# The first attention's K and V products in five passes of 128 and 64 rows in place of six of 96

## The reference, cut to what matters

```python
x = x + _L0_xattn_ref(_layernorm(x), ctx_768, Wq, bq, Wk, bk, Wv, bv, Wo, bo)
# in _L0_xattn_ref: 16 heads of 16 channels, Nkv = 361
q = (query @ Wq + bq).reshape(B, Nq, H, D).transpose(0, 2, 1, 3)
k = (key_value @ Wk + bk).reshape(B, Nkv, H, D).transpose(0, 2, 1, 3)
v = (key_value @ Wv + bv).reshape(B, Nkv, H, D).transpose(0, 2, 1, 3)
attn = jnp.clip(jnp.einsum('bhqd,bhkd->bhqk', q, k) * scale, -CLAMP, CLAMP)
attn = jax.nn.softmax(attn, axis=-1)
attn = jnp.where(jnp.any(jnp.isnan(attn)), 1.0 / Nkv, attn)
x = jnp.einsum('bhqk,bhkd->bqhd', attn, v).reshape(B, Nq, Cq) @ Wo + bo
```

## Time and profile before

| | |
|---|---|
| median of 3 runs | 946.31 us (946.12 to 947.51) |
| the profiled execution | 947.37 us |
| its span, first to last instruction | 945.5 us |
| PE busy in the span | 792.7 us (84%) |
| DVE, ACT, POOL busy | 708.9, 559.2, 298.9 us |
| mean granted clock of TensorE | 0.910 of full speed |

### The profile page before, as it was taken

One profiled execution on the slowest core, in us unless ns is written; L12 is line 12 of the kernel. 1 busy time (PEld: TensorE's weight loads), 2 busy tenths in 40 slices (PEclk: granted clock), 3 DMA queues, 4 the chain that ended last, 5 costly groups with the idle time before them and its releaser, 6 DMA issues.

```text
span 945.5 us, 22076 instructions
## 1 busy us (share of the span) xinstructions
PE 792.7 (84%) x8198; PEld 582.7 (62%) x8198; DVE 708.9 (75%) x1450; ACT 559.2 (59%) x1159; POOL 298.9 (32%) x258
## 2 busy tenths in 40 slices
PE   3777888889898768999889999997655999769994
PEld 2455666666665645777657777784213887459994
DVE  8678777877877888777476666654796998677866
ACT  6666666666665436634365555536897776673542
POOL 6166444444441506040232220002730221342400
PEclk9699999999999776999999999997557999789998
DMA  6423444344452246515076554455210000200002
GB/s 169 108 70 86 113 96 99 103 97 114 119 121 81 80 138 222 175 35 145 23 222 188 170 168 146 124 135 142 75 42 11 1 1 1 90 1 2 2 2 70
DMA packets 76898, 89.53 MB, mean 95 GB/s; under 512 B 22150, under 2 KB 64929, under 8 KB 76826
## 3 DMA queue, kind: packets, MB, share of 16 engines
q1 hardware_dynamic: 69994, 80.50, 30.6%
q0 software_dynamic: 6144, 7.42, 3.0%
q10 hardware_dynamic: 688, 0.66, 0.3%
HBM read 72.87 MB, written 15.43 MB: 93 GB/s over the span
## 4 chain that ended last, share of the span: by engine, by line
PE 53%; DVE 26%; ACT 9%; issue 8%; POOL 2%; DMA 1%; ACTq 0%; DVEq 0%; POOLq 0%
PE ps L1207 11%; PE ps L1194 10%; PE ps L581 4%; PE ps L379 3%; PE ps L477 3%; PE ps L551 3%; DVE p L567 3%; PE ps L623 3%; PE ps L532 2%; PE ps L2229 2%; DVE m L537 2%; PE ps L2240 2%; DVE pmax L1681 1%; ACT area L2039 1%; PE ps L1728 1%
## 5 line engine op out<-in xcount | busy, mean ns | idle before, releaser
L537 DVE TENSOR_REDUCE m<-ps 100x2 f32<-100x722 f32 x128 | 115.6, 904 | 51.6 <-PE ps L532 49.7
L558 ACT ACTIVATE p<-ps 128x800 f32<-128x800 f32 x128 | 106.8, 834 | 41.6 <-PE ps L551 38.6
L1256 ACT ACTIVATE hT<-ps,cols 128x500 f32<-128x500 f32 (+1 forms) x96 | 62.5, 651 | 103.3 <-PE ps L1194 103.1
L1263 DVE TENSOR_TENSOR hT_l<-hT,hT_h 128x500 f16<-128x500 f32 (+1 forms) x96 | 62.4, 652 | 59.1 <-ACT hT_h L1257 59.1
L567 DVE SCALAR_TENSOR_TENSOR p<-p 128x600 f32<-128x600 f32 x128 | 106.6, 834 | 0.0
L1207 PE MATMUL ps<-w_h,hT_h 128*125 128x256 f16 (+1 forms) x384 | 104.7, 273 | 1.8 <-DVE x L1303 1.2
L1207 PE MATMUL ps<-w_h,hT_l 128*125 128x256 f16 (+1 forms) x384 | 104.7, 273 | 0.0
L1207 PE MATMUL ps<-w_l,hT_h 128*125 128x256 f16 (+1 forms) x384 | 104.7, 273 | 0.0
L1099 POOL DMA_INDIRECT xe<-tokens,slot_of x32 | 43.2, 1349 | 151.4 <-PE ps L1217 102.1
L1194 PE MATMUL ps<-xe_h,w_h 128*128 128x500 f16 (+1 forms) x192 | 73.3, 382 | 15.8 <-DVE xe_l L1237 5.5
L551 PE MATMUL ps<-qs,ks 128*128 128x100 f16 x768 | 63.3, 212 | 14.7 <-ACT p L558 14.7
(11 more groups left out here) (348 smaller groups left out, 2101.6 us busy)
## 6 DMA issues: line engine op xcount, KB each, us to landing
sw<-in_L_ffn_w_dram SPq DMA_DIRECT2D x16, 512.0 KB, 6.8
sw<-in_L_ffn_w_dram SPq DMA_DIRECT2D x8, 1024.0 KB, 5.8
k_parts<-kp SPq DMA_DIRECT2D x32, 192.0 KB, 2.2
ks<-k_parts SPq DMA_DIRECT2D x32, 192.0 KB
stage<-in_L_xattn_W_f_dram SPq DMA_DIRECT2D x6, 1024.0 KB, 7.5
ctx_f<-in_ctxT_dram SPq DMA_DIRECT2D x16, 270.8 KB, 3.2
stage<-in_ctxT_dram SPq DMA_DIRECT2D x8, 541.5 KB, 8.6
area<-in_ctxT_dram SPq DMA_DIRECT2D x16, 270.8 KB, 6.1
```

The costliest lines, as they stand in the source:

```text
L537: v.tensor_reduce(m32[p][:, 2 * i:2 * i + 2], ps[0:T, at:at + 2, 0:KV], AX.X, ALU.max).then_inc(m_max, 1)
L558: s.activation(p32[:, i % HALF, :, :, :].rearrange("p j n t -> p n j t"), ps[:, t_bank(i):t_bank(i) + 2, 0:(KJ + 1) * T].rearrange("p n (j ...
L1256: s.activation(hT[:, f % 3, 0:m], bank[2 + f % 2][:, 0:m], ACT.Silu, bias=bias, scale=1.0 / WS)
L1263: v.tensor_tensor(hTp[p][1][:, f, 0:m], hT[:, f % 3, 0:m], hTp[p][0][:, f, 0:m], ALU.subtract).then_inc(f_l, 1)
```

## The change

The 192 channels are cut into 128 and 64 in place of 96 and 96. The first 128 keep a high tile `ctxh[p][:, 0, :]` and a low tile `ctxl[p]`. The last 64 are loaded twice, into rows 0 to 63 and 64 to 127, and the tile `ctxh[p][:, 1, :]` holds their high part in the upper and their low part in the lower half of its rows; with the last 64 rows of the weights' high part standing twice as well, one pass of 128 rows makes high by high and high by low. Low by high for these channels is a pass of its own, over rows 0 to 63. That makes five passes: four of 128 rows and one of 64.

To write both halves of that tile with one subtraction, ACT writes the rounded copy into the lower rows of a tile `ctx_rest` alone, whose upper rows DVE sets to zero at the start; POOL subtracts it from the f32 value. As there is one `ctx_rest` for both buffers, `c_scalar` now waits for POOL's subtractions of the batch before. The guard's products take all 128 rows for the first part and rows 64 to 127 for the second. Wk, Wv and the context come in two transfers each, and the counts that wait for them double.

```diff
-        for name, rows_ in (("Wq", 128), ("Wk", KC), ("Wv", KC), ("Wo_heads", 128)):
+        for name, rows_ in (("Wq", 128), ("Wk", 128), ("Wv", 128), ("Wo_heads", 128)):
-        ctxp = [[sba(f"ctx{n}{p}", [KC, 2, KV], F16) for n in "hl"] for p in range(2)]
+        ctxh = [sba(f"ctxh{p}", [128, 2, KV], F16) for p in range(2)]
+        ctxl = [sba(f"ctxl{p}", [128, KV], F16) for p in range(2)]
+        ctx_rest = sba("ctx_rest", [128, KV], F16)
...
+        REST = CK - 128
+        def lower_rows(w):
+            return w[128:CK, :][None, :, :].broadcast_to((2, REST, C))
+        def ctx_terms(w, p):
+            hi, lo = w
+            return ((hi[:, 0, :], ctxh[p][:, 0, :]), (lo[:, 0, :], ctxh[p][:, 0, :]), (hi[:, 1, :], ctxh[p][:, 1, :]),
+                    (hi[:, 0, :], ctxl[p][:, :]), (lo[0:REST, 1, :], ctxh[p][0:REST, 1, :]))
...
-            for k in range(2):
-                for i, j in TERMS:
-                    mm = pe.matmul(at[:, 0:KV], wk[i][:, k, c * 128:(c + 1) * 128], ctxp[p][j][:, k, :],
-                                   start=(n == 0), stop=(n == 5))
+            for n, (w, src) in enumerate(ctx_terms(wk, p)):
+                mm = pe.matmul(at[:, 0:KV], w[:, c * 128:(c + 1) * 128], src, start=(n == 0), stop=(n == 4))
...
-                for k in range(2):
-                    for i, w in TERMS:
-                        mm = pe.matmul(at[0:v_rows(j), j % 2 * C:(j % 2 + 1) * C],
-                                       ctxp[p][i][:, k, j * AT:j * AT + v_rows(j)], wv[w][:, k, :],
-                                       start=(j != 1 and n == 0), stop=(n == 5), skip_group_check=True)
+                for n, (w, src) in enumerate(ctx_terms(wv, p)):
+                    mm = pe.matmul(at[0:v_rows(j), j % 2 * C:(j % 2 + 1) * C], src[:, j * AT:j * AT + v_rows(j)], w,
+                                   start=(j != 1 and n == 0), stop=(n == 4), skip_group_check=True)
...
             if c == 0:
-                s.wait_ge(ctx_in[p], 16 * (t + 1))
+                s.wait_ge(ctx_in[p], 32 * (t + 1))
                 wait(s, v_mm, 2 * (b - 1))
-            s.activation(ctxp[p][0][:, c, :], ctx_f32[p][:, c, :], ACT.Copy,
-                         accum_out=ctx_sum[:, c, bass.ds(b, 1)]).then_inc(c_h, 1)
+            else:
+                wait(s, c_l, 2 * b)
+            of = slice(0, 128) if c == 0 else slice(REST, 128)
+            high = ctxh[p][:, 0, :] if c == 0 else ctx_rest[of, :]
+            s.activation(high, ctx_f32[p][of, c, :], ACT.Copy, accum_out=ctx_sum[of, c, bass.ds(b, 1)]).then_inc(c_h, 1)
...
-            g.tensor_tensor(ctxp[p][1][:, c, :], ctx_f32[p][:, c, :], ctxp[p][0][:, c, :], ALU.subtract).then_inc(c_l, 1)
+            high = ctxh[p][:, 0, :] if c == 0 else ctx_rest[:, :]
+            parts = ctxl[p][:, :] if c == 0 else ctxh[p][:, 1, :]
+            g.tensor_tensor(parts, ctx_f32[p][:, c, :], high, ALU.subtract).then_inc(c_l, 1)
...
-            sp.dma_start(ctx_f32[p][:, :, :], ctx_d[b] ...).then_inc(ctx_in[p], 16)
+            sp.dma_start(ctx_f32[p][:, 0, :], ctx_rows[b][0:128, :]).then_inc(ctx_in[p], 16)
+            sp.dma_start(ctx_f32[p][:, 1, :], ctx_rows[b][128:CK, :][None, :, :].broadcast_to((2, REST, KV))
+                         ).then_inc(ctx_in[p], 16)
...
             for n in range(H):
                 row_ = HR * (n % 4)
                 for k in range(2):
+                    of = slice((0, REST)[k], 128)
                     mm = pe.matmul(UB_[row_:row_ + D, n // 4 * B:(n // 4 + 1) * B],
-                                   w_in_["Wv"][0][:, k, n * D:(n + 1) * D], ctx_sum[:, k, :],
+                                   w_in_["Wv"][0][of, k, n * D:(n + 1) * D], ctx_sum[of, k, :],
...
+            v.memset(ctx_rest[0:REST, :], 0.0)
             vs.inc(v.memset(eps_col[:, :], LN_EPS))
...
+                    s.dma_start(raw[:, 0, :], src[0:128, :]).then_inc(w_in[name], 16)
+                    s.dma_start(raw[:, 1, :], lower_rows(src)).then_inc(w_in[name], 16)
```

More of the change, by code:

```diff
@@ L149, in bias_row_tensor @@
         def bias_row_tensor(pe, part):
-            pe.wait_ge(wvo_in, 32)
+            pe.wait_ge(wvo_in, 48)
             for k in range(2 * part, 2 * part + 2):
@@ L250, in build @@
         ctx_raw = sba("ctx_f32", [128, 2, 2, KV])
-        ctx_f32 = [ctx_raw[0:KC, p, :, :] for p in range(2)]
-        ctxp = [[sba(f"ctx{n}{p}", [KC, 2, KV], F16) for n in "hl"] for p in range(2)]
+        ctx_f32 = [ctx_raw[:, p, :, :] for p in range(2)]
+        ctxh = [sba(f"ctxh{p}", [128, 2, KV], F16) for p in range(2)]
+        ctxl = [sba(f"ctxl{p}", [128, KV], F16) for p in range(2)]
+        ctx_rest = sba("ctx_rest", [128, KV], F16)
         k32 = [sba(f"k32_{c}", [128, KV]) for c in range(CC)]
@@ L290, in build @@
         qk_sum = sba("qk_sum", [128, 4, B])
-        ctx_sum = sba("ctx_sum", [KC, 2, B])
+        ctx_sum = sba("ctx_sum", [128, 2, B])
         guard = sba("guard", [128, 4])
@@ L315, in build @@
         ctx_d = a["ctxT"].rearrange("(c p) (b k) -> b p c k", c=2, b=B)
+        ctx_rows = a["ctxT"].rearrange("c (b k) -> b c k", b=B)
+        REST = CK - 128
[5 more added lines that the diff above has]
+                    (hi[:, 0, :], ctxl[p][:, :]), (lo[0:REST, 1, :], ctxh[p][0:REST, 1, :]))
         TERMS = ((0, 0), (0, 1), (1, 0))
@@ L353, in split_weight @@
             else:
-                v.wait_ge(w_in[name], 16)
+                v.wait_ge(w_in[name], 32)
                 vs.inc(v.tensor_scalar(hi, src, WS, None, ALU.mult))
@@ L375, in k_tensor @@
             turn_free(pe, free)
-            n = 0
-            for k in range(2):
-                for i, j in TERMS:
-                    mm = pe.matmul(at[:, 0:KV], wk[i][:, k, c * 128:(c + 1) * 128], ctxp[p][j][:, k, :],
-                                   start=(n == 0), stop=(n == 5))
-                    n += 1
+            for n, (w, src) in enumerate(ctx_terms(wk, p)):
+                mm = pe.matmul(at[:, 0:KV], w[:, c * 128:(c + 1) * 128], src, start=(n == 0), stop=(n == 4))
             mm.then_inc(k_mm, 1)
@@ L646, in c_scalar @@
             if c == 0:
-                s.wait_ge(ctx_in[p], 16 * (t + 1))
+                s.wait_ge(ctx_in[p], 32 * (t + 1))
                 wait(s, v_mm, 2 * (b - 1))
-            s.activation(ctxp[p][0][:, c, :], ctx_f32[p][:, c, :], ACT.Copy,
-                         accum_out=ctx_sum[:, c, bass.ds(b, 1)]).then_inc(c_h, 1)
+            else:
[3 more added lines that the diff above has]
+            s.activation(high, ctx_f32[p][of, c, :], ACT.Copy, accum_out=ctx_sum[of, c, bass.ds(b, 1)]).then_inc(c_h, 1)
         def c_gpsimd(g, b, p, c):
             g.wait_ge(c_h, 2 * b + c + 1)
-            g.tensor_tensor(ctxp[p][1][:, c, :], ctx_f32[p][:, c, :], ctxp[p][0][:, c, :], ALU.subtract).then_inc(c_l, 1)
+            high = ctxh[p][:, 0, :] if c == 0 else ctx_rest[:, :]
+            parts = ctxl[p][:, :] if c == 0 else ctxh[p][:, 1, :]
+            g.tensor_tensor(parts, ctx_f32[p][:, c, :], high, ALU.subtract).then_inc(c_l, 1)
         def context_load(sp, b, p):
             wait(sp, c_l, 2 * (b - 1))
-            sp.dma_start(ctx_f32[p][:, :, :], ctx_d[b] if isinstance(b, int) else
-                         ctx_d[bass.ds(b, 1)].rearrange("o p c k -> (o p) c k")).then_inc(ctx_in[p], 16)
+            sp.dma_start(ctx_f32[p][:, 0, :], ctx_rows[b][0:128, :]).then_inc(ctx_in[p], 16)
+            sp.dma_start(ctx_f32[p][:, 1, :], ctx_rows[b][128:CK, :][None, :, :].broadcast_to((2, REST, KV))
+                         ).then_inc(ctx_in[p], 16)
         def a_tensor(pe, b, t, p):
@@ L2493, in _ @@
             for name in ("Wk", "Wq", "Wv"):
-                raw = w_in_[name][0]
-                s.dma_start(raw[:, :, :], a[f"L0_xattn_{name}"].rearrange("(k p) n -> p k n", k=raw.shape[1])
-                            ).then_inc(w_in[name], 16)
+                raw, src = w_in_[name][0], a[f"L0_xattn_{name}"]
+                if name == "Wq":
+                    s.dma_start(raw[:, :, :], src.rearrange("(k p) n -> p k n", k=2)).then_inc(w_in[name], 16)
+                else:
+                    s.dma_start(raw[:, 0, :], src[0:128, :]).then_inc(w_in[name], 16)
+                    s.dma_start(raw[:, 1, :], lower_rows(src)).then_inc(w_in[name], 16)
             s.wait_ge(vchain, 1)
@@ L2619, in x_load @@
                 sp.dma_start(x[:, LB * g:LB * (g + 1), :], x_all[:, LB * g:LB * (g + 1), :]).then_inc(x_in[g], 16)
-            sp.dma_start(ctx_f32[0][:, :, :], ctx_d[0]).then_inc(ctx_in[0], 16)
+            context_load(sp, 0, 0)
             x_load(0)
@@ L2629, in _ @@
             sp.dma_start(rows[:, :], a["rows"]).then_inc(const_in, 16)
-            sp.dma_start(ctx_f32[1][:, :, :], ctx_d[1]).then_inc(ctx_in[1], 16)
+            context_load(sp, 1, 1)
             for g in range(1, LG):
@@ L2647, in _ @@
             k_store(sp, 1, 0, 1, 0)
-            sp.wait_ge(wvo_in, 16)
+            sp.wait_ge(wvo_in, 32)
             raw = w_in_["Wo_heads"][0]
```

## The result

The changed kernel takes **981.07 us** (975.03 to 984.54), the kernel before 946.91 (946.12 to 947.94) beside it; the ratio is 1.0353, 95% interval [1.0293, 1.0413]. Slower, as forecast, but by 34 us where I had 5. The profiled execution took 984.54 us, with a span of 982.7. Two single runs that were far slower than the others of their kernel, 1188.59 us with plain loads and 1548.92 us of the kernel before, are left out of all that follows.

A forecast was written before the change was run, and what follows sets the result against it. PE was taken to bound the kernel, with K and V products setting the first attention's period. Loop +1.3, guard +3.7 and opening 0 gave +5.0 us on the 946.31 median: 951.3 us, own range 948 to 956.

The forecast's parts named there:

- The opening: Start of the kernel, before the loop: extra memset, first K group and larger loads together 0, with -0.2 to +1.0 us.
- Edits at nothing: SP's extra transfer per batch (0.45 us), the ACT and POOL splits and c_scalar's new wait: all covered, no cost.
- The guard: Guard's column sums (L857): 32 changes of height make 0.6 us into 4.3, +3.7 us; bounds 0 and +6.1.
- The loop: First attention's batches: K products save 1.8 us, V products lose 3.1 to 64-row switches, +1.3 us in all.
- No drain at 64 rows: Rival: K, V and guard products run on without switch cost, 8.6 us less, 937.7 us; chance 0.14.
- None in the guard: Rival: 64-row products drain in the loop but not in the guard's sums, +1.3, 947.6 us; chance 0.09.
- A dearer drain: Rival: each switch costs the whole 0.165 us, +8.9 in the loop, +6 in the guard, 961 us; chance 0.05.

The follow-up runs named there:

- plain loads: Changed kernel with each doubled load (context, Wk, Wv) split into two loads of 64 rows: 961.16 us, ratio 1.0217.
- full height: Changed kernel with fifth pass and guard's second product over all 128 rows: 945.66 us with each doubled load split in two, 972.24 us with doubled loads kept.
- guard in two runs: Changed kernel with doubled loads split in two and the guard's products ordered by height, one change in place of 31: 957.97 us, ratio 1.0123.
- rows first: Changed kernel with no 64-row products and doubled loads' source written (64, 2, row) in place of (2, 64, row): 944.15 us, ratio 0.9983.
- the kernel before with the guard's edit: Kernel before, with every second product of the guard's sums taking 64 rows in place of 96: 953.73 us, ratio 1.0076.

## Why the prediction was right in direction and wrong in size

- **The step that failed: "The opening ... All together 0, with -0.2 to +1.0 if the loads come later than that."** I costed the larger loads by their bytes at the 230 GB/s of the stretch; that rate belongs to transfers spread over many engines, and the new ones ran at some 45 to 50. It cost 18.0 us ahead of the first copy, of which 16.3 go with plain loads (92.5 to 76.2); at full height 13.4 us go by the order of the source alone (89.2 to 75.8).
- **"Edits at nothing. SP issues one more transfer per batch (0.45 us)".** Its issue was covered; what the transfer does to others was not. Where xn's loads come beside it, m's rows and q's land late: 5.3 us in steps 11 and 12, of which 4.7 go with plain loads (40.1 to 35.4).
- **The guard**, +3.7: the sums cost +4.1, right. The clock that falls behind them was not in the sum; with it the step is 5.8 us longer in the kernel before, 7.5 in the changed one.
- **The loop**, +1.3: 0.09 and 0.10 us per change of height are right, but the sum gives 0.11 us a step, and 18.01 (guard in two runs) against 17.64 are 0.37. The chain before, then with the guard in two runs:

```profile
107.84 0.65 PE ps L581 x24
...
111.83 0.36 PE ps L551 x8
```

```profile
164.42 0.72 PE ps L588 x24
...
167.06 1.58 PE ps L486 x10
168.64 0.46 PE ps L558 x8
```

  K's five take 0.98 and 0.99, 0.10 less a step than before (forecast 0.13). V's ten with the scores behind them take 2.04 where 1.84 stood (1.48 in the earlier trace rows, and 0.36), 0.20 more (forecast 0.16); V's last five with theirs 1.27 where 1.15 stood, 0.12 more (forecast 0.08). The attention-value products ahead of K's second half take 0.07 more, which I had at nothing. That is some 0.3; under 0.1 us a step stays unassigned. Step 1, where I had V's length hidden behind POOL, grew by 1.9 us with plain loads. I had the saving at 0.64 a step without drains, and full height shows it (17.00).
- **Rivals.** *No drain at 64 rows* falls: 64 rows pay, 96 don't. *None in the guard* falls with its 4.68 us. *A dearer drain* falls on 0.09 to 0.11. None of the four had the transfers in it.
- **The direction** does not rest on the loads alone: with plain loads the kernel is still some 2% slower, and the guard and the loop, the two terms of my sum, are the larger part of that.

The terms, taken out one after the other by the medians: doubled loads 19.9 us (981.07 to 961.16), the guard's order 3.2 (to 957.97; 5.9 by its step), the remaining products of 64 rows 12.3 (to 945.66), which is the kernel before again (945.96 beside it). The three runs with plain loads spread over 11 us, so the first two numbers are known to a few us only. At full height the loop's saving of 5.8 us in steps 2 to 10 (9 x 0.64) goes into a later first copy (4.5) and a longer step 1 (3.0); part of the last is DVE's stall beside POOL (a clip of 4.61 us, 2.32 before). Taken out last, the doubled loads are worth 27 to 28 us (972.24 to 945.66 with plain loads, to 944.15 with rows first), more than taken out first, since in the loop the drains had covered part of them. Open: why the first copy comes anywhere from 75 to 79 us in kernels without doubled context loads, why the guard's step takes 17.5 to 19.5 us at full height, and why the part behind the loop varies by 9 us.

## What to carry to other kernels

Cost a new transfer by the engines that its access pattern reaches, not by its bytes: a source with its two copies in front ran here at a fifth of the rate, and swapping its first two dimensions cured it at the same bytes. Where a contraction doesn't fill the rows, run the short pass at full height with zeros or a harmless extra term, or put all short products side by side; 0.2 us a pair had eaten the whole saving. Follow a stall into the clock behind it, and the next engine that it touches, before the sum is closed.

## What the runs showed that I had not expected

- A load whose source has its two copies in front leaves stretches of 45 GB/s at a DMA share of 0.14; with the copies behind the rows the first 9 us of the same stretch move 161 to 324 GB/s.
- After 4.7 us of 16-column products that drained between heights, TensorE's granted clock was 0.59 over the next 10 us in the changed kernel, and 0.66 (301.41 to 311.15 us) in the kernel before with the guard's edit; with the same products in two runs it stayed at 1.00.
- A DVE instruction of 8 columns took 0.16 us, or 2.3, or 4.6, by where POOL's additions of 1,024 columns stood beside it. The Trainium skill, "SBUF — State Buffer", section SBUF: two separate sides, calls the port pair of the two an exclusive lock held for a whole instruction; the trace agrees in that the clip ends where the additions end (83.37 and 83.35 us), and there it stood through two of them, of some 2.9 us each, not one.
